# Four small transfers on GpSimd's queue, statistics two slots later, and a gate chain one chunk earlier, in an eight-layer transformer kernel

## The reference, cut to what matters

```python
x = x + L0_xattn(ln(x), ctx, ctx)          # 16 heads of 16, relu on q, k, v      -> stage a0
x = x + L0_ffn(ln(x))                      # 8 experts, the best one, hidden 64   -> stage f0
x = x + L1_xattn(ln(x), ctx, mask)         # 16 heads, key mask, both layer norms -> stage a1
x = x + L1_ffn(ln(x))                      # 4 of 16 experts, hidden 1024         -> stage f1
x = x + L2_xattn(ln(x), ctx)               # 16 heads                             -> stage a2, units 0 to 15
x = x + L2_ffn(ln(x))                      # causal attention, then a mixture     -> stage a2, units 16 to 31, then f2
x = x + L3_xattn(ln(x), ctx)               # 8 heads of 64                        -> stage a4
x = x + L3_ffn(ln(x))                      # one quantised matrix                 -> stage q8
```

## Time and profile before

| | |
|---|---|
| median of 3 runs | 3414.13 us (3412.98 to 3415.45) |
| the profiled execution: time, span | 3417.49 us, 3415.5 us |
| TensorE busy | 2817.4 us, 82% of the span |
| VectorE, ScalarE, GpSimd busy | 1984.2, 1653.9, 942.6 us (58%, 48%, 28%) |
| mean granted TensorE clock | 0.908 |
| transfers from SP's queue / from GpSimd's | 168.62 MB / 16.79 MB |

### The profile page before, as it was taken

How to read it: one execution, slowest core, us unless ns; L and a number is a source line. 1 busy time by engine, 2 the same in 40 slices (tenths; PEclk the granted TensorE clock), 3 DMA queues, 4 the chain that set the end, 5 groups by cost and what they waited for, 6 DMA issues and landing times. The chain is left out here.

```text
span 3415.5 us, 69558 instructions
## 1 busy us (share of the span) xinstructions
PE 2817.4 (82%) x25927; PEld 1902.6 (56%) x26046; DVE 1984.2 (58%) x4533; ACT 1653.9 (48%) x3032; POOL 942.6 (28%) x863
## 2 busy tenths in 40 slices
PE   5988675888869999999969999996139958999993
PEld 2554353455436666666635556664138945776772
DVE  4777554778655444443358887776714344555547
ACT  2777332666634444444427776665325523333331
POOL 5441005666100000000043334340440043443413
PEclk8999897899979999999979999998569978999995
DMA  3221002111025000000011211110323334323301
GB/s 112 74 74 54 13 1 76 64 61 64 31 65 162 1 1 1 1 1 1 1 58 62 66 55 44 46 49 12 137 97 92 94 97 85 79 68 78 75 20 49
DMA packets 195461, 189.86 MB, mean 56 GB/s; under 512 B 25968, under 2 KB 173696, under 8 KB 194976
## 3 DMA queue, kind: packets, MB, share of 16 engines
q1 hardware_dynamic: 188992, 168.62, 16.7%
q0 software_dynamic: 6144, 16.79, 1.5%
HBM read 67.09 MB, written 41.42 MB: 32 GB/s over the span
## 5 line engine op out<-in xcount | busy, mean ns | idle before, releaser
L1541 DVE TENSOR_TENSOR f1H<-f1HF,f1H 128x512 bf16<-128x512 f32 x256 | 176.6, 692 | 398.2 <-ACT f1H L1386 398.2
L1341 PE MATMUL ps<-f1w,f1H 128*128 128x256 bf16 x3072 | 378.5, 273 | 0.0
L1319 PE MATMUL ps<-f1xT,f1w 128*128 128x512 bf16 x1448 | 358.7, 383 | 11.9 <-ACT f1H L1386 5.9
L1341 PEld LDWEIGHTS ps<-f1w,f1H 128*128 128x128 bf16 x3072 | 301.5, 98 | 90.4 <-issue 1.1
L1383 ACT ACTIVATE f1HF<-ps 128x512 f32<-128x512 f32 x256 | 152.8, 597 | 333.9 <-PE ps L1319 333.8
L732 ACT ACTIVATE a2PT<-ps 128x512 f32<-128x512 f32 (+1 forms) x512 | 255.6, 543 | 56.0 <-PE ps L570 34.3
L1319 PEld LDWEIGHTS ps<-f1xT,f1w 128*128 128x128 bf16 x1536 | 148.1, 98 | 150.6 <-issue 16.4
L547 PE MATMUL ps<-a2KS,a2QS 49*128 49x256 bf16 (+1 forms) x1024 | 172.8, 262 | 44.5 <-DVE a2NM L849 19.6
L849 DVE TENSOR_REDUCE a1NM<-ps 128x2 f32<-128x512 f32 x256 | 165.5, 685 | 53.3 <-PE ps L547 53.1
L849 DVE TENSOR_REDUCE a0NM<-ps 128x2 f32<-128x512 f32 x256 | 165.4, 685 | 47.4 <-PE ps L547 47.4
L849 DVE TENSOR_REDUCE a2NM<-ps 128x2 f32<-128x512 f32 x256 | 165.6, 685 | 26.1 <-PE ps L547 24.6
(11 more groups left out here) (508 smaller groups left out, 6802.0 us busy)
## 6 DMA issues: line engine op xcount, KB each, us to landing
a2KS<-a2KH SPq DMA_DIRECT2D x192, 64.0 KB
a2QS<-a2QH SPq DMA_DIRECT2D x192, 64.0 KB
a4KS<-a4KH SPq DMA_DIRECT2D x96, 128.0 KB
a4QS<-a4QH SPq DMA_DIRECT2D x96, 128.0 KB
slots<-zeros SPq DMA_DIRECT2D x1, 9984.0 KB, 32.0
f2XS<-slots SPq DMA_DIRECT2D x39, 256.0 KB
results<-f2XS SPq DMA_DIRECT2D x39, 256.0 KB, 2.1
f1WF<-in_f_w SPq DMA_DIRECT2D x32, 256.0 KB, 2.7
```

Of the source, the lines that this page charges most:

```text
L1319: m = nc.tensor.matmul(ps[:, (u * NCH + i) % 2, :], w1[:, x, kt, i * P:i * P + P], xT[:, half, y, kt, :], start=(j == 0), stop=(j == len(t ...
L1341: m = nc.tensor.matmul(out, H[:, (u * NCH + i) % HR, x, t * P:t * P + P], w2[:, y, i, :], start=first, stop=(f == YC - 1 and j == 2 and no ...
L1541: nc.vector.tensor_tensor(H[:, (u * NCH + i) % HR, 1, :], HF[:, (u * NCH + i) % 2, :], H[:, (u * NCH + i) % HR, 0, :], SUB).then_inc(S["h_ ...
```

## The change

Three parts, in one edit.

1. The four transfers of `maxT` are issued by GpSimd in place of SP, in all attention stages, behind the same two waits on the maxima's parts.
2. In `slots()` the statistics move from slot 0 to slot 2, which puts them behind `maxT` (slot 1) on GpSimd's queue and, on VectorE, between the row maxima of slots 2 and 3. The loading and splitting of the second half's weights in a2 hang on the same entry and move with it, three times in all.
3. In f0, `xT` of both halves stands in chunk 0, `route` and `gate` in chunk 1, `stats` in chunk 2, `sel` and then `apply` in chunk 3. The four small products with `tri` in the gate chain become one of 128x256.

```diff
@@ slots() @@
         put(1, "maxT", "c", 0)
         put(0, "xT", "a", 0)
-        put(0, "stats", "z", 0)
+        put(2, "stats", "z", 0)
@@ SyncE's loop: taken out @@
-                    elif name == "maxT":
-                        sp.wait_ge(S["m_hi"].sem, S["m_hi"].at(u, 1))
-                        sp.wait_ge(S["m_lo"].sem, S["m_lo"].at(u, 1))
...
-                                sp.dma_start(dst, MH[j * n:j * n + n, u % 2, half, :]).then_inc(M.sem, 16)
@@ GpSimd's loop: put in, behind "stats" @@
+                    elif name == "maxT":
+                        pool.wait_ge(S["m_hi"].sem, S["m_hi"].at(u, 1))
+                        pool.wait_ge(S["m_lo"].sem, S["m_lo"].at(u, 1))
...
+                                nc.gpsimd.dma_start(dst, MH[j * n:j * n + n, u % 2, half, :]).then_inc(M.sem, 16)
@@ ffn, plan() @@
         def early(u, k):
-            k = k if paired else k // 2
+            if paired:
+                if u + 1 < UNITS:
+                    yield from ((("xT", u + 1, 0), ("xT", u + 1, 1)), (("route", u + 1, 0), ("gate", u + 1, 0)),
+                                (), (("sel", u + 1, 0),))[k]
+                if u + 2 < UNITS and k >= 2:
+                    yield ("stats" if k == 2 else "apply", u + 2, 0)
+                return
+            k = k // 2
...
@@ ffn, gate() @@
-                    for t in range(UT):
-                        v = nc.vector.tensor_tensor(EQ[:, t], EQ[:, t], g["tri"][:, 0:NE, 0:E], MUL)
-                    link(v)
+                    if NE == E:
+                        lower = g["tri"][:, 0:NE, 0:E]
+                        link(nc.vector.tensor_tensor(EQ[:], EQ[:], lower.rearrange("p (one n) e -> p one n e", one=1
+                                                                                 ).to_broadcast([P, UT, NE, E]), MUL))
```

More of the change, by code:

```diff
@@ L467, in _ @@
                             other_constants()
+                    elif name == "maxT":
+                        pool.wait_ge(S["m_hi"].sem, S["m_hi"].at(u, 1))
+                        pool.wait_ge(S["m_lo"].sem, S["m_lo"].at(u, 1))
+                        if u == 0:
+                            pool.wait_ge(S["const_ready"].sem, S["const_ready"].at(0, 4))
+                        n = NH // 2
+                        for half in range(2):
+                            for j in range(2):
+                                if wide:
+                                    dst = QS[WIDE_MAX + half:WIDE_MAX + half + 1, u % RING, 1, j * n:j * n + n, :]
+                                else:
+                                    dst = QS[64 * j + MAXROW + half:64 * j + MAXROW + half + 1, u % RING, 0, :, :]
+                                nc.gpsimd.dma_start(dst, MH[j * n:j * n + n, u % 2, half, :]).then_inc(M.sem, 16)
                     elif name == "fin":
@@ L1103, in early @@
                     yield ("apply", u + 2, 0)
-                if u + 1 < UNITS and paired:
-                    yield ("sel", u + 1, 0)
         made = [("stats", 0, 0), ("apply", 0, 0), ("gates", 0, 0)]
@@ L1437, in gate @@
                     link(nc.vector.tensor_tensor(EQ[:], every, own, ALU.is_equal))
-                    for t in range(UT):
-                        v = nc.vector.tensor_tensor(EQ[:, t], EQ[:, t], g["tri"][:, 0:NE, 0:E], MUL)
-                    link(v)
+                    if NE == E:
+                        lower = g["tri"][:, 0:NE, 0:E]
+                        link(nc.vector.tensor_tensor(EQ[:], EQ[:], lower.rearrange("p (one n) e -> p one n e", one=1
+                                                                                 ).to_broadcast([P, UT, NE, E]), MUL))
+                    else:
+                        for t in range(UT):
+                            v = nc.vector.tensor_tensor(EQ[:, t], EQ[:, t], g["tri"][:, 0:NE, 0:E], MUL)
+                        link(v)
                     link(nc.vector.tensor_tensor(CMP[:], CMP[:], EQ[:], ADD))
```

## The result

| | before | after |
|---|---|---|
| median | 3414.13 us | 3396.28 us (3394.68 to 3400.51) |
| the profiled execution: time, span | 3417.49, 3415.5 us | 3396.89, 3395.1 us |
| mean granted TensorE clock | 0.908 | 0.914 |

The ratio of the medians is 0.9949, with a 95% interval of 0.9934 to 0.9963: 0.5% faster. 3399 was predicted, with 3374 to 3418 as the range. A sum that comes out proves little here, since its terms have both signs and their errors can cancel. So this table splits each profiled execution at the first TensorE instruction of each stage; the length of a stage, in us, reaches to the start of the next. It holds all kernels of this study. What they are is told with the experiments.

What follows compares the result with a forecast made beforehand. TensorE was taken as busiest, held up by Q's rows at slot 0 and f0's masks. Terms -15 + 12 + 8 + 0 - 20 = -15 us took 3417.5 to 3402.5 profiled, 3399 for the median, range 3374 to 3418.

Steps and rivals of the forecast that it cites:

- the loop through slot 0: Attention stages: K's issues, then Q's on SP, Q's landing, then the next period; slot 0 waits 27.6 us in a0.
- the displaced K in a1: a1, VectorE: the moved statistics stand ahead of the masked keys, which start 1.0 us later, and K's low part follows.
- the cover at slot 8: a2: maxima issued by GpSimd land in 5.9 us, within the 7.35 us before the transposed scores, so the move is hidden.
- a0, -15: Stage a0: earlier issue of K, K's low part 0.3 us earlier and less half clock save 15 us (0 to 27.6).
- a1, +12: Stage a1: moved statistics delay the masked keys and the loop, 0.9 us a period, costing 12 us (0 to 18).
- a2, +8: Stage a2: statistics between two row maxima delay a product by 0.45 us, 0.2 in the causal units: 8 us (0 to 13).
- a4, 0 (-3 to +3): Stage a4: after its first units K and Q land well ahead of slot 0, so no change, bounds -3 and +3.
- GpSimd, 0, by an issue of 1.26 us: GpSimd's queue: the four added issues, taken at 1.26 us each, stay hidden before slot 8 and cost 0.
- f0, -20: Stage f0: the earlier gate chain removes TensorE's wait for the masks, 16.6 us, and some half clock: -20 (-12 to -25).
- the two gaps are even: f0: the second transposition's new bank wait, about 1.4 us, is offset by the route product no longer waiting for it.
- The third rival: Little comes of the gains: a0 gives only 5 us, f0 14, so 3415 us, no change; chance 0.18.
- The second: Rival: the moved statistics cost nothing in a1 and a2, so -35 us, 3379 us; chance 0.17.
- No wait of line 559 for `MH`: Sign for the forecast in the profile after: the transposed scores of slot 8 never wait for the maxima's transfers.

Runs made afterwards that it cites:

- e3_stats: The kernel before with only the statistics moved from slot 0 to slot 2, the maxima's transfers still on SP: 3427.27 us, ratio 1.004.
- e1_f0: The kernel before with only the third part of the change, the new order in f0 and the joined product with `tri`: 3388.16 us, ratio 0.992.
- e7_bank: On top of e1_f0, f0's second transposition moved from chunk 0 to between the two products of chunk 1: 3373.18 us, ratio to before 0.9902.
- e2_split: The kernel before with the maxima's transfers on GpSimd, VectorE's statistics in slot 0, GpSimd's part in slot 2 behind the transfers: 3399.9 us, ratio 0.994.
- e8_eight: The kernel after with each of the four transfers of the maxima cut into two, eight issues on GpSimd: 3424.57 us, ratio to before 1.0044.
- e5_ahead: The kernel before with the maxima's transfers on GpSimd and the statistics in slot 0 on both engines, so GpSimd normalises first: 3623.5 us, ratio 1.0634.
- e4_mix: The kernel after with VectorE's statistics back in slot 0 in a1 and a2, GpSimd's part still in slot 2: 3375.4 us, ratio to before 0.988.

## Why the prediction was right, term by term

The terms against the stages (a0, a1, a2, a4 with q8, f0): -12.8, +16.0, +7.1, -7.1 and -23.6, together -20.4 us of span, where I had -15. The four parts of the mechanism that the forecast rests on held: the loop through slot 0, the displaced K in a1, the cover at slot 8, the gate chain in f0. That the medians differ by 17.9 us where I had 15 is in part luck, since the errors have both signs: a1 cost 4 more than its term, a0 gave 2 less, f0 4 and a4 7 more.

- *a0, -15: measured -12.8.* Averaged over units 3 to 15, a period took 18.32 us before and 17.39 after. Of the 0.93, K's low part behind the period's start is 0.58 (6.99 to 6.41; 6.6 to 6.3 in undisturbed units, which is the 0.3 that I took, and the rest is that fewer of them are at half clock). K's delay on SP is 0.34 (0.40 to 0.06). I took 0.4 in 15 units although left only nine with a delay; it came near since two of the delays were 1.3 and 1.5 us, which is luck. The two causes share something, which I had added: in e3_stats K's delay went too (0.08), with SP's queue unchanged, since the maxima left earlier. By single executions the queue alone gives 6, the statistics alone 11, both 13. The kernels that have a0 in the same form put the queue at 5 (332 in the mean of before, e1_f0 and e7_bank, 327.4 in e2_split), the statistics at 10 and both at 11 (320.5, 321.7 and 319.5), known to some 2 to 4 us.
- *a1, +12: measured +16.* The masked keys are late by 0.94 us in undisturbed periods, as predicted. The size was too small because a period with a longer wait more often starts at half clock: there K's low part comes at 11.0 to 11.4 us behind the start and not at 9.9, in seven of 15 units (in one of them the first product, at 668.91, took 2.37 us in place of 1.47). On average it is 10.36 against 9.33, 1.03 us in 15 periods. The execution of before had the longest a1 of the six kernels with on-time transfers and the statistics in slot 0 (404.0 to 408.4), so the cost may be as much as 20, past my bound of 18.
- *a2, +8: measured +7,* by the rows of the mechanism that I named (TensorE's wait for `a2NM` 19.6 to 24.2). It was 0.15 us in units 16 to 31, where I had 0.2, and 0.3 in the first half, where I had 0.45.
- *a4, 0 (-3 to +3): measured -7: wrong.* This is the one term that failed: I counted that K and Q land well ahead of slot 0, and passed over the first units. (TensorE's attention there is 12 us shorter, of which 5 go again before q8 starts.) In units 1 to 4, where K's and Q's rows land right before they are wanted, a4 is as a0: TensorE's wait for Q's rows in a4 was 15.2 us and is 9.8. Unit 1 takes 19.9 to 20.3 us in all seven kernels in which GpSimd issues the maxima ahead of its normalisation, and 22.4 to 23.1 in the four with the maxima on SP, so some 2.7 us are the queue's. Most of the rest is unit 3 alone. Its windows, from its predecessor's first row maximum to its own, in before, e1_f0 and e7_bank (maxima on SP), and in after and e8_eight (on GpSimd); the clock is the third number from the end:

```profile
2865.90:2899.60 33.70, 32.02 (x215) 23.09 (x214) 15.66 (x38) 13.10 (x24) 10.45 (x10) 0.85 0.32 72
```
```profile
2837.30:2873.40 36.10, 34.40 (x215) 24.16 (x214) 15.69 (x38) 13.09 (x24) 10.45 (x10) 0.79 0.29 67
```
```profile
2829.30:2858.30 29.00, 27.35 (x216) 19.95 (x214) 15.65 (x38) 12.96 (x24) 10.45 (x10) 1.00 0.36 83
```
```profile
2848.60:2876.80 28.20, 26.62 (x206) 19.24 (x204) 15.67 (x38) 12.46 (x24) 12.61 (x14) 1.00 0.37 85
```
```profile
2871.20:2904.30 33.10, 31.45 (x216) 22.88 (x214) 15.68 (x38) 13.10 (x24) 14.68 (x18) 0.87 0.31 73
```

  The same work takes 28 to 29 us where the clock stays up and 33 to 36 where it falls for a part, and both happen with either queue, though not equally often. With the maxima on SP it fell in three of four kernels (before, e1_f0, e3_stats), with them on GpSimd ahead of the normalisation in one of seven (e8_eight); it fell in e5_ahead as well. What tips it is open. So about 3 us of a4's gain are shown as the change's, and more is likely but not shown: a4 with q8 is 646.9 us in the mean of the four, and 641.7 over the six others with four issues.
- *GpSimd, 0, by an issue of 1.26 us:* the term was right and its price wrong, on the safe side: 0.52 us, landing 1.1 us behind the end of the last one. In the middle it is 3.9 us from the low part to the landing, where I had 5.9. From issue to landing it was 1.7 us. The Trainium skill's first byte after about 1 us (DMA: Bandwidth & Descriptors, Specifications) has room in that, but no row shows a first byte by itself. What held the forecast together was the order on the queue, as e5_ahead shows, more than the room. In a stage's last two periods the room is 3 to 4 us and the 3.9 just fill it or overrun it, as e8_eight and the waits beside it show.
- *f0, -20: measured -23.6,* -26.4 alone. The wait went by 16.9 us (16.6 taken). That the two gaps are even held: 11 us more for the bank, against waits of up to 1.72 us of the route product in each unit before. Of the other 6.7 us, where I had 3 or 4, TensorE's busy time in f0 gives 5.4 (131.67 to 126.28 for nearly the same instructions), which is work that ran at half clock behind those waits and now doesn't.

The third rival (little comes of the gains, 3415) fell with a0 and f0, although its sign, a new wait of TensorE for `xT` in f0, did appear: the route product's wait went in exchange. The second (statistics free, 3379) fell as a forecast, but 3375 is what e4_mix gives, where they are left in their gap.

Of the signs for the forecast, the wait for `SELP` (4.2 us), the late masked keys and the longer a1 came as said. The slot-0 wait of a0 fell by a third and not by half, since part of the gain is faster work. "No wait of line 559 for `MH`" was too strict: there is one at the end of a0, a1 and a2, before as after.

## What to carry to other kernels

When an instruction group is moved on one engine, ask in each stage that shares the schedule which gap it leaves and what stands behind its new place: the same slot gave 11 us in a0 and took 17 in a1, and a slot by stage kept the one without the other. Where transfers move to a compute engine's queue, their place in that engine's program can cost far more than their issue (here 6.6% from e2_split to e5_ahead, against 0.9% for twice the issues), and the room that hides them has to be read where a stage fills and empties too. And a wait that goes may leave a smaller one at the next handover: e7_bank found 9 us in the one that was "even".

## What the runs showed of the hardware

- A direct transfer of 4 KB issued by GpSimd took 0.52 us, four in 2.19 us; SP took 2.77 for the same four. Of 320 such issues in the kernel after (a4's 64 are of 2 KB), the longest took 0.74 us, while single issues of K and Q on SP (0.59 us in the middle) took up to 2.04.
- After waits of a few microseconds TensorE's clock is at times 0.5 for the work that follows (after 4.66 us, 1.93 in place of 1.07 us for sixteen products of the same form), so such a wait costs more than its length. In a4's unit 3 the same work ran with or without such a stretch, 4 to 8 us apart.
- Once, in e8_eight, GpSimd's first transfer left 3.7 us behind its data with the engine idle. It was not seen in the kernel after.
